# An attention and mixture-of-experts block on one core: shared-expert tiles read x from the router's transposed copy, 18 of them placed ahead of the routed tiles and 14 behind, and late pairs stored plainly

## What is computed

```python
x = x + attn(layernorm(x))                       # 32 heads of 16 features, plus a memory read
h = layernorm(x)
scores = sigmoid(h @ router_w.T)                 # 16 experts
_, topk_idx = top_k(scores + e_bias, 4)
topk_w = scores[topk_idx] / sum(scores[topk_idx])
routed = sum over the 4: topk_w * (silu(g) * u) @ down.T      with g, u = h @ gate_up.T (192 each)
shared = silu(h @ shared_gate.T) * (h @ shared_up.T) @ shared_down.T
out = x + routed + shared
```

## Time and profile before

| | us |
|---|---|
| median of 3 runs (1951.1 to 1951.97) | 1951.28 |
| the profiled execution | 1949.25 |
| its span, from first to last instruction | 1947.2 |
| attention alone (to the first `gate_up` at 1098.25) | 1098 |
| pairs 0 to 9 | 98 |
| routed pairs 10 to 81 | 674 |
| late pairs, joins and last stores | 77 |

### The profile page before, as it was taken

How to read it: one execution, slowest core, us unless ns; L and a number is a source line. 1 busy time by engine, 2 the same in 40 slices (tenths; PEclk the granted TensorE clock), 3 DMA queues, 4 the chain that set the end, 5 groups by cost and what they waited for, 6 DMA issues and landing times.

```text
span 1947.2 us, 34879 instructions
## 1 busy us (share of the span) xinstructions
PE 1870.6 (96%) x9240; PEld 965.5 (50%) x9241; DVE 1023.7 (53%) x1989; ACT 981.8 (50%) x1919; POOL 926.8 (48%) x1131
## 2 busy tenths in 40 slices
PE   6799999999999999999999899999999999999996
PEld 5444445444544454445333455555555555555553
DVE  5667777878787878787887152122211221222212
ACT  3366776677667767776776532223332232322321
POOL 3532566666667766774643550333333333333333
PEclk9799999999999999999999999999999999999998
DMA  6423234534453345333542797777777777777779
GB/s 193 111 67 83 64 95 131 149 98 107 130 151 100 104 129 153 100 96 114 150 148 72 275 343 231 183 142 141 141 143 144 141 141 142 145 141 144 140 163 218
DMA packets 158488, 275.61 MB, mean 142 GB/s; under 512 B 28640, under 2 KB 64736, under 8 KB 155552
## 3 DMA queue, kind: packets, MB, share of 16 engines
q0 software_dynamic: 41392, 106.96, 26.8%
q1 hardware_dynamic: 108688, 147.61, 26.6%
q10 hardware_dynamic: 8288, 19.58, 2.9%
HBM read 143.55 MB, written 136.27 MB: 144 GB/s over the span
## 4 chain that ended last, share of the span: by engine, by line
PE 86%; ACT 5%; DVE 3%; DMA 2%; issue 2%; SPq 1%; POOL 1%; DVEq 0%; POOLq 0%
PE ps_gu L1907 23%; PE ps_pv L1210 12%; PE ps_exp L1197 10%; PE ps_max L1183 9%; PE ps_y L1926 7%; PE ps_misc L1103 5%; PE ps_y L1930 5%; PE ps_x L1886 4%; ACT prob L723 3%; DVE mx L973 2%; PE ps_misc L1128 2%; PE ps_misc L1152 2%; PE ps_misc L1223 1%; PE ps_misc L1074 1%; PE ps_misc L1117 1%
## 5 line engine op out<-in xcount | busy, mean ns | idle before, releaser
L973 DVE TENSOR_REDUCE mx<-ps_max 128x2 f32<-128x1024 f32 x512 | 618.1, 1219 | 172.5 <-PE ps_max L1183 158.5
L723 ACT ACTIVATE prob<-ps_exp 128x512 f32<-128x512 f32 x1024 | 583.9, 597 | 154.1 <-PE ps_exp L1197 136.6
L1197 PE MATMUL ps_exp<-qs,ks 98*128 98x512 bf16 x1024 | 391.8, 384 | 24.0 <-ACT prob L723 19.9
L1907 PE MATMUL ps_gu<-wts_sb,xT 128*128 x1152 | 402.7, 493 | 1.3 <-issue 1.1
L1611 POOL DMA_INDIRECT out<-yt,idx x72 | 111.9, 1554 | 467.8 <-ACT yt L1680 453.7
L1183 PE MATMUL ps_max<-ks,qs 96*128 96x512 bf16 x1024 | 308.7, 383 | 9.0 <-DVE mx L973 4.9
L1784 DVE COPY hT<-ps_h 128x384 f32<-128x384 f32 x88 | 49.1, 558 | 467.9 <-PE ps_h L1916 467.9
L1907 PEld LDWEIGHTS ps_gu<-wts_sb,xT 128*128 128x128 f32 x1152 | 207.3, 190 | 170.6 <-issue 56.1
L1210 PE MATMUL ps_pv<-prob,vs 128*32 128x512 f32 x2048 | 249.8, 601 | 0.0
L1670 ACT ACTIVATE gs<-ps_gu 128x192 f32<-128x192 f32 x176 | 58.3, 331 | 373.4 <-PE ps_gu L1907 373.4
L1197 PEld LDWEIGHTS ps_exp<-qs,ks 98*128 98x128 bf16 x1024 | 99.6, 98 | 209.3 <-ACT prob L723 101.3
(11 more groups left out here) (192 smaller groups left out, 2146.7 us busy)
## 6 DMA issues: line engine op xcount, KB each, us to landing
xt<-rows_by_expert SPq DMA_DIRECT2D x144, 264.5 KB, 2.8
dnr_sb<-in_dnr SPq DMA_DIRECT2D x144, 128.0 KB, 2.6
qk_parts<-parts POOLq DMA_DIRECT2D x112, 120.0 KB, 3.5
qs<-qk_parts SPq DMA_DIRECT2D x64, 192.0 KB, 3.1
wts_sb<-in_wts ACTq DMA_DIRECT2D x12, 1024.0 KB, 7.0
x_sb<-in_x SPq DMA_DIRECT2D x16, 512.0 KB, 4.5
qs<-qk_parts SPq DMA_DIRECT2D x64, 128.0 KB, 3.1
x_plus_memory<-am SPq DMA_DIRECT2D x16, 512.0 KB, 5.1
```

The source lines that it names most:

```text
L723: act.activation(prob[:, s, q], ps_exp[:, q % 2], ACT.Exp, scale=SCALE).then_inc(s_exp, 1)
L973: dve.tensor_reduce(mx[:, k % 2, 4 * s + 2 * p:4 * s + 2 * p + 2], ps_max[:, p], AX_X, ALU.max).then_inc(s_maxd, 1)
L1197: pe.matmul(ps_exp[:, q % 2], ks[0:ROWS + MROWS, kk, s * P:(s + 1) * P], qs[0:ROWS + MROWS, kk, q], start=True, stop=True).then_inc(s_sc, 1)
L1907: mm = pe.matmul(ps_gu[:, i, 0:2 * I], xT[:, i, d], w, start=(d == 0), stop=(d == DC - 1))
```

## The change

`xn2T` gets the layout [partition, tile, chunk, column] and SP stores it (`store_xn2T`) into a new area `xn2_transposed` in place of the rows of `xn2`. Shared tiles load x from there, already transposed, and `gate_up` takes it from `xt` directly. The transposes of x on PE and the copies on ACT are left out for the 16 shared pairs. The slot of x is free only when `gate_up` has read it, so `load_x` now waits for `gate_up` of the pair (`s_gu`) tile by tile, where it waited for the pair's transposes. ACT may write `xn2T` of the next unit only after the store of this one has landed: a new wait in `xn2T_out`, and POOL's wait in `norm2` goes. `EARLY` is 18: pairs 0 to 8 are early, 9 to 80 routed, 81 to 87 late, seven of them. The weights of experts 12 and 13 move from pair 8 to pair 7. The constants `jrow` are loaded at pair 4 and not 3. Of the late pairs only the first adds into `out` in DRAM. The other six load both sums (12 loads of 512 KB where there were 5), DVE adds them (`both_sums`, before for the last pair only), and ACT stores the result (`store_late`). Joins are 10 where there were 12.

```diff
-EARLY = 20
+EARLY = 18
...
-    xn2T = lent("xn2T", [P, DC, UT])
+    xn2T = lent("xn2T", [P, 2, DC, P])
...
+        def store_xn2T(c):
+            wait(s_xn2T, 2 * c + 2)
+            sp.dma_start(XN2T[c], xn2T[:, :, :, :].rearrange("p t c j -> p t (c j)")).then_inc(s_xn2st[c % 2], 16)
...
+                if k == 0 and b >= 4:
+                    store_xn2T(b - 4)
+                if k == 2 and b == NB:
+                    store_xn2T(NU - 3)
...
-                    if b >= 3:
-                        store_xn2(b - 3)
...
-                store_xn2(NU - 2)
                 store_x2(NU - 1)
+                store_xn2T(NU - 2)
             if n == 2:
-                store_xn2(NU - 1)
+                store_xn2T(NU - 1)
...
-                wait(s_xn2st[c % 2], 16 * (c // 2))
...
+                if t == 0 and c > 0:
+                    act.wait_ge(s_xn2st[(c - 1) % 2], 16 * ((c - 1) // 2) + 16)
+                    act.sem_inc(s_acf, 1)
                 act.wait_ge(s_xn2Tp, 2 * c + t + 1)
-                act.activation(xn2T[:, :, t * P:(t + 1) * P], ps_misc[:, :].rearrange("p (c t) -> p c t", c=DC),
+                act.activation(xn2T[:, t], ps_misc[:, :].rearrange("p (c t) -> p c t", c=DC),
...
-            self.summed = known and h >= H1 + 2
+            self.both = known and h > H1
...
-    WEIGHTS_AT = {0: 2, 1: 3, 2: 4, 4: 5, 8: 6, H0 + 3: 7}
+    WEIGHTS_AT = {0: 2, 1: 3, 2: 4, 4: 5, 7: 6, H0 + 3: 7}
...
-        def load_x(pair):
+        def load_x(last, pair):
+
             for i in range(2):
+                if last.exists and last.kind == SHARED:
+                    wait(s_gu, 2 * last.h + i + 1)
                 if pair.kind == SHARED:
-                    sp.dma_start(xt[:, pair.slot(i), 0:D], XN2[bass.ds(pair.t[i], 1)].rearrange("o p d -> (o p) d")).then_inc(
-                        s_x[pair.slot(i)], 16)
+                    sp.dma_start(xt[:, pair.slot(i), 0:D], XN2T[pair.t[i] // 2, :, i]).then_inc(s_x[pair.slot(i)], 16)
...
-                wait(s_xp, 2 * pair.h + 2)
                 if pair.kind == ROUTED:
+                    wait(s_xp, 2 * pair.routed + 2)
...
-                load_x(later)
-            for n, h in enumerate((0, 1, 2)):
+                load_x(pair, later)
+            for n, h in enumerate((0, 1, 3)):
                 if is_at(pair, h):
                     chain(n)
-            if is_at(pair, 3):
-
-                all_of("logits", "x2_stored", "o_added")
+            if is_at(pair, 4):
+
+                all_of("logits", "x2_stored", "xn2_stored", "o_added")
...
-        def load_sum(o, n, to, s):
+                           max_dma_last_dim=8192).then_inc(s, 16)
+
+        def load_sums(n):
             t = EARLY + 2 * n
-            pool.dma_start(sums[:, to], SUM[o][t * P:(t + 2) * P].rearrange("(t p) d -> p t d", p=P)).then_inc(s, 16)
-
-        def add_late(pair):
-            if not pair.summed:
-
-                wait(s_join[pair.h - H1], 16)
+            for o in range(2):
+                rows = SUM[o][t * P:(t + 2) * P].rearrange("(t p) d -> p t d", p=P)
+                pool.dma_start(sums[:, (LATE // 2) * o + n], rows).then_inc(s_sl[n], 16)
+
+        def add_first_late(pair):
+            wait(s_join[0], 16)
             for i in range(2):
                 wait(s_y, 2 * pair.h + i + 1)
-                pool.dma_start(rows_of(SUM[0], pair.t[i]), late_y(pair, i), accum_op=ALU.add).then_inc(s_lst[pair.slot(i)], 16)
+                pool.dma_start(rows_of(SUM[0], pair.t[i]), late_y(pair, i), accum_op=ALU.add).then_inc(s_lst[i], 16)
 
         wait(s_yp, H1)
-        load_sum(1, 2, 2, s_sl[2])
-        for n in range(2):
-            join(EARLY + 2 * n, n)
-        load_sum(1, 3, 3, s_sl[3])
-        for m in range(LATE // 2 - 1):
-            for t in (4 * m, 4 * m + 2):
-                join(t, 2)
-            if m == 1:
-                for n in range(4, LATE // 2):
-                    load_sum(1, n, n, s_sl[n])
-            if m == 2:
-                load_sum(0, LATE // 2 - 1, 0, s_sl0)
-            add_late(Pair(H1 + m, (H1 + m) // 2, (H1 + m) % 2))
+        load_sums(1)
+        join(EARLY, s_join[0])
+        load_sums(2)
+        early = iter(range(0, EARLY, 2))
+        for n in range(3, LATE // 2):
+            for t in (next(early), next(early)):
+                join(t, s_join[1])
+            if n == 4:
+                add_first_late(Pair(H1, H1 // 2, H1 % 2))
+            load_sums(n)
+        for t in early:
+            join(t, s_join[1])
...
+        def store_late(pair):
+            for i in range(2):
+                act.wait_ge(s_y, 2 * pair.h + i + 1)
+                act.sem_inc(s_acg, 1)
+                act.dma_start(rows_of(SUM[0], pair.t[i]), late_y(pair, i)).then_inc(s_last, 16)
...
-            if following.exists:
+            if following.exists and following.kind == ROUTED:
...
-            if before.exists and not before.summed:
+            if before.exists and not before.both:
...
+            if before.both:
+                store_late(before)
...
-        x_out(Pair(0, 0, 0))
...
+        def both_sums(pair):
+            n = pair.h - H1
+            dve.wait_ge(s_sl[n], 32)
+            dve.tensor_tensor(sums[:, n], sums[:, n], sums[:, LATE // 2 + n], ALU.add).then_inc(s_both, 1)
...
-            if pair.h == H2 - 1:
-                dve.wait_ge(s_both, 1)
-            else:
-                dve.wait_ge(s_sl[n], 16)
+            dve.wait_ge(s_both, n)
...
-            if before.exists and before.summed:
+            if before.both:
+                both_sums(before)
                 y_sum(before)
```

73 lines of the change are left out of this document (32 added, 41 removed).

## The result

The changed kernel takes 1965.05 us (median of 4 runs, 1962.89 to 1965.81); the kernel before took 1951.62 in the same session (4 runs, 1951.1 to 1953.33). The ratio is 1.0067, with a 95% interval of 1.0056 to 1.0079: slower by 0.67%, where I had forecast 0.17% and a range that ended at 1962. The profiled execution is the one of 1962.89 us; its span is 1961.1, 13.9 more than before (1947.2).

A forecast was written before the change was run, and what follows sets the result against it. PE was taken to bound the kernel, except before the first routed pair (x behind pads) and at the end (POOL's queue). Early stage 0, routed -1.8, end +5.0: +3.2 us, 1952.5 profiled, 1954.5 against the median; range 1945 to 1962.

The forecast's parts named there:

- Transposes cost 0.88 us a pair: Shared pairs on PE: the eight transposes of x take 0.88 us for each pair, 14.1 us over 16 pairs.
- If PE alone set the early stage, the first routed gate_up would come at 1182.4: Early stage, bound by PE only: first routed gate_up at about 1182.4, a gain of 14; said not to be reached.
- SP starts its pads at about 1151 and the second group at 1160: Early stage, SP's queue: pads wait behind pair 5's gate_up, starting at about 1151, not 1147.9; second group at 1160.
- Weights 12 and 13 push the last pads back by 5 us: Early stage: 2.1 MB of weights on ACT's queue delay SP's last pads by about 5 us, to 1186.
- A clock of 0.5 costs 2.5 us: Before the first routed gate_up: after PE's wait the granted clock falls to 0.5, costing 2.5 us.
- Early stage: 0: Up to the first routed gate_up, forecast at 1196.5: gain 0, with bounds of 14 and -3.
- Attention: 1 us: Attention, unit 13: ACT's copy waits for unit 12's store and PE waits for ACT; 1 us taken.
- Routed part and what follows it: -1.8: 72 routed pairs at the same pace; 0.9 us earlier to the first late pair, 0.9 more to the last routed addition.
- End: +5.0: After the last routed addition: 2.6 us more DMA work and 2.4 us more tail; the end grows by 5.
- weights do not hold the pads: Rival, early stage: pads not delayed, clock stays; first routed gate_up at 1189 to 1191, kernel 1947 to 1949; chance 0.18.
- late pairs at PE's pace: Rival, end: late pairs go at PE's pace, end 3 shorter instead of 5 longer, 1946.5; chance 0.12.
- the third rival: End: DVE waits early for sums and PE behind it; end grows by 10 to 13, 1959.5 to 1962.5; chance 0.18.

The follow-up runs named there:

- a_early20: Changed kernel with the split of the kernel before, 20 shared tiles early and 12 late, plain late stores kept; ratio 1.0005 to the kernel before.
- a_all: Changed kernel with weights 4 and 5 later, weights 12 and 13 at pair 8, pads ahead of x loads, ten PE instructions; 1944.34 us, ratio 0.9963.
- a_weights_later: Changed kernel, but ACT sends the weights of experts 4 and 5 after the first silu of pair 1; 1968.31 us, ratio 1.0051 to the kernel before.
- a_pads_first: Changed kernel, but on SP the six pads of pairs 5 and 6 stand ahead of the loads of x for pairs 7 and 8; ratio 1.0051.
- a_weights8: Changed kernel, but the weights of experts 12 and 13 are sent at pair 8, not pair 7; ratio 1.0015 to the kernel before.

## Why the routed pairs take 5 us more

PE's loop does the same work in both kernels; its code differs only in how it waits and in the registers for that. What differs is where it lies: its first instruction is PE's 14168 before and 14030 after. So I moved it, with instructions at the very start of PE's program that only count up a semaphore:

```
         def _(pe):
+            for _ in range(10):
+                pe.sem_inc(s_steps, 1)
             experts["tensor"](pe)
```

> The changed kernel with 10 more instructions at the very start of PE's program, which only count up a semaphore that nobody reads. They move the loop of routed pairs in PE's instruction stream from instruction 14030 to 14040; in the kernel before it begins at 14168, and both 14168 and 14040 leave the same rest when divided by 128. Theory: the 0.1 to 0.45 us that PE loses at the top of nearly each of the 32 passes (7.9 us over the routed part, 1.8 in the kernel before) hang on where the loop's code lies in memory. Then the routed part falls from 679.1 to 673 to 675 us and the time to about 1959.5. Rival: they come from what the loop holds now (waits counted from the first routed pair need other registers) or from another engine; then the routed part stays 679 and the time 1965.

Routed part 672.5 us, 6 pairs late by 1.0 us together. The loss is gone, with ten instructions *added*. PE's waits from 1210 to 1870 in this run:

```profile
PE ps_gu L1919 <- issue: 0.3, 1, 0.3
```

The time was 1964.02 us against 1959.94 on its chip (I had expected 1959.5), ratio 1.0013 (0.9998 to 1.0027), where the changed kernel had 1.0067. The early stage of the profiled execution happened to be 3.9 us longer than in the changed kernel (residual at +21.0, POOL's wait for `xm_sb` 7.5 us for 6.1), for which I have no reason.

The other side of the test is to make the kernel before slow.

> The kernel before with 6 more instructions at the start of PE's program, which only count up a semaphore nobody reads; its loop of routed pairs then begins at PE's instruction 14174 instead of 14168, so that the rest by 16 is 14, as in the changed kernel (14030), where it was 8. In the changed kernel the loop cost 7.9 us at 14030 and 1.0 at 14040. Theory: it is the place of the loop's code, whatever the kernel, and what counts in it is the place within a piece of 16 instructions. Then the routed part grows from 673.9 to 678 to 680 us and the time by about 5 us. Rival: the place within a larger piece counts (14174 leaves 30 by 64 and 94 by 128, 14030 leaves 14 and 78), or the loss needs the changed kernel's loop; then the routed part stays within 1.5 us of 673.9.

Six instructions (14174) did nothing: 673.6 us, ratio 0.9995 (0.9983 to 1.0006), so it is not the place within 16 instructions, as I had thought. With 118 the loop begins at 14286:

> The kernel before with 118 counting instructions at the start of PE's program: its loop begins at PE's instruction 14286, which leaves 78 by 128, as 14030 in the changed kernel does. With 6 (14174) the routed part had stayed 673.6 us, so a rest of 14 by 16 is not what makes the loop slow. Theory: the place within a piece larger than 16 instructions counts, whatever the kernel. Then the routed part grows to 678 to 680 us, with 25 or more of 72 pairs late. Rival: the loss needs what the changed kernel's loop holds, together with its place; then 672 to 675 us.

Routed part 680.2 us, 28 pairs late by 8.0 us together, time 1966.25 against 1950.1: ratio 1.0089 (1.0068 to 1.0109). Only 6.2 of the 16 us are the loop. About 8 are the counting instructions themselves: PE's first matmul began at 18.96 us and not at 11.05, behind "issue" and no longer behind DVE, and the attention ended 9.8 us later. (With 6, 10 and 64 of them, in b_pe6, a_pe10 and a_pe64, it still began at 10.8 to 10.9.) The kernel *before*, with nothing changed in its work, has the changed kernel's loss in the loop. Its PE waits from 1210 to 1870:

```profile
PE ps_gu L1907 <- issue: 5.5, 22, 0.6
```

The first matmul, PE's timeline in this run and in the kernel before:

```profile
18.96 1.09 PE L1255 MATMUL ps_misc<-identf,xn 128*128 128x128 f32 x4 [18.96 <-issue]
```
```profile
11.05 1.09 PE L1255 MATMUL ps_misc<-identf,xn 128*128 128x128 f32 x4 [11.05 <-DVE xn L1008]
```

> The changed kernel with 64 counting instructions at the start of PE's program: its loop begins at PE's instruction 14094, which leaves 14 by 64 as 14030 does, but 14 by 128 where 14030 leaves 78. Theory (pieces of 64 instructions or of a part of 64): routed part 678 to 680 us, as without them. Rival (pieces of 128 or more, or a few hot places only): 672 to 675 us.

At 14094 the routed part took 673.2 us: the theory that a rest by 64 decides it is refuted. In all, of the places of the loop's start, 13988, 14040, 14094, 14168 and 14174 gave 672 to 674 us in ten profiled executions, 14030 and 14286 gave 678 to 680 in eight. The two slow ones lie exactly 256 apart. The Trainium skill, "Advanced Engine Details and Errata", section "ISA Cache", says that a sequencer's instruction cache has lines of 256 instructions. By that rule both slow places are the same place in a line (206) and each fast one is another (164, 216, 14, 88, 94), with which the runs agree. They do not single out 256: counted by 128 the two slow places are alike as well (78), and no fast one is (36, 88, 14, 88, 94). Nor does the rule say why 206 is slow and 216 is not, when the loop of 219 instructions crosses a line's end from both, and no run here tells that. Shown is that the place alone makes and removes the loss; what in the place does it stays open.

## What the end waits for

**Without the joins of the early tiles.** Nine joins are left out, so the rows of the early tiles in out lack their second sum.

```
             for t in (next(early), next(early)):
-                join(t, s_join[1])
+                pass
...
-        for t in early:
-            join(t, s_join[1])
```

> The changed kernel without the nine joins (out += second sum, 0.5 MB each) of the early tiles, which POOL issues among the loads of sums: it leaves these additions out, so the early tiles' rows of out lack their second sum. It measures what the end of the kernel waits for. Theory: from POOL's first load of a sum to the end (60.7 us) the transfers on POOL's queue set the time, joins among them; without them DVE no longer waits 20 us for sums, and the stretch falls to what PE needs for the seven late pairs, 50 to 53 us, the time to 1954 to 1957. Rival: the sums come as late without the joins, because the loads' own bytes and the routed additions set them; then it stays at 58 us or more.

From the first load of a sum to the end it took 50.0 us, 10.7 less, and the one wait of DVE for a sum there is 0.3 us. The time was 1953.69 us, ratio to the kernel before 1.0021 (1.0010 to 1.0032). So it is the joins, and the loads of sums behind them on POOL's queue, that set the last 60 us of the changed kernel; PE's pace would allow 50.

```profile
DVE wts_sb L1836 <- DMA wts_sb<-second_sum_rows: 0.3, 1, 0.3
```

**Split and stores apart.** In three executions (before, b_pe6, b_pe118) the late code of the kernel before took 58.2, 60.2 and 60.1 us, so the 2.5 of the two first profiles say little. Four kernels on one chip, the two splits with either late stage. The old late stage is put back word for word (joins and accumulating stores for the first two late pairs, accumulating stores over one loaded sum for the next, both sums for the last); its core:

```
-        load_sums(1)
-        join(EARLY, s_join[0])
-        load_sums(2)
+        load_sum(1, 2, 2, s_sl[2])
+        for n in range(2):
+            join(EARLY + 2 * n, n)
+        load_sum(1, 3, 3, s_sl[3])
...
+            add_late(Pair(H1 + m, (H1 + m) // 2, (H1 + m) % 2))
```

> The changed kernel once more, on one chip with the next three: split 18/14, plain late stores. The theory that the bytes and kinds on POOL's queue set the late stage (joins 0.203, loads 0.375 MB a us): 60 to 61.5 us from POOL's first load of a sum to the end, with the old late stage at the same split 1 to 3 us more (PE needs seven pairs, and eleven joins' and twelve additions' work comes to 31 us more than its loads). Rival: the late code makes no difference at all, 0.5 us or less between the two.

> The changed kernel with the late stage of the kernel before at the split 18/14: two late pairs added by joins and accumulating stores, five over sums, all accumulating but the last pair. Theory of POOL's queue: 11 joins and 12 accumulating additions of 0.262 MB are 8.9 MB at 0.203, 43.9 us, and its 6 loads of sums, 6 of x and 2 stores 5.2 MB at 0.375, 14 us: 57.9 us, as much as the plain one (57.7), so 60 to 62 us to the end. Rival (the plain stores cost): under 59 us.

> The changed kernel with 20/12, plain late stores, on the same chip: 11 joins and 2 additions accumulate (6.3 MB, 31.0 us), 10 loads of sums, 5 of x, 10 stores are plain (9.2 MB, 24.5 us): 55.5 us, 2.2 less than at 18/14. Theory: the stretch to the end is 1 to 2 us shorter than in after_2. Rival: a late pair less gives PE's 8.5 us, over 5.

> The changed kernel with 20/12 and the late stage of the kernel before: the work on POOL's queue is that of the kernel before, 55.1 us, so by the theory the stretch is within 1 us of that of a_early20_2. Rival: PE's late pairs without transposes (8.47 for 9.34 us) end it earlier: 3 us or more shorter.

From the first load of a sum to the end:

| | plain late stores | the old late stage |
|---|---|---|
| 18 and 14 | 61.2 (after_2) | 64.3 (a18_old_late) |
| 20 and 12 | 59.6 (a_early20_2) | 60.8 (a20_old_late_2) |

An earlier run of the last one gave 60.9:

> The changed kernel with the split 20 and 12, and with the late stage of the kernel before put back (two late pairs added by joins and accumulating stores, one load of a sum each for the next, two for the last): against the run with 20 and 12 alone it takes the plain late stores away. PE's loop begins at the same instruction (13988) in both. There the routed additions' end (POOL's first load of a sum, 1899.5) to the end of the span was 59.7 us with 15.3 less of PE's work, and in the kernel before 58.2. Theory: that stretch is set by the bytes and kinds of POOL's transfers, not by PE. Then it takes 58 to 59 us here, though PE's pairs take 8.47 us where they took 9.34, so the plain stores cost about 1.2 us. Rival: PE's shorter pairs let the old late stage end earlier; the stretch takes 54 us or less, and the plain late stage has cost over 5 us.

That run had been forecast at 58 to 59 us, with the plain stores as a cost of 1.2; its time was 1959.47 us, ratio 1.0045 (1.0030 to 1.0061), where a_early20 had 1.0005. So the plain stores are a gain, 3.1 us at the split for which they were made and 1.2 at the other, and the split costs 1.6 with them (3.5 without). The 64.3 is one execution, 2.3 above the highest of nine with plain stores. At 20 and 12 it is two against two (60.8 and 60.9 against 59.6 and 59.7), where the forecast had them within 1. Which of the kernels ends how is seen at PE: with the old stage at 18 and 14 it is through at 1948.4, 18 us before the end, while POOL's last additions went out at 1944.84 only; with the plain one it is through at 1956.2, 5 us before. PE's last row in each:

```profile
1947.29 1.13 PE L1947 MATMUL ps_y<-sdnr_sb,hT 64*128 64x512 f32 x4
```
```profile
1954.10 2.08 PE L1942 MATMUL ps_y<-sdnr_sb,hT 64*128 64x512 f32 x4
```

My estimate of equal work for the two at 18 and 14 (57.9 against 57.7 us, so 60 to 62 to the end) missed that an accumulating store can only be sent when its y is there: POOL stood idle for 5.9 and 6.7 us ahead of its last two pairs of them, waiting for DVE.

## Both kernels beaten

The three edits on the pads and the ten instructions together:

> All four together on the changed kernel: weights of experts 4 and 5 after the first silu of pair 1, weights 12 and 13 at pair 8, pads ahead of the loads of x, 10 instructions ahead on PE. Theory: singly they gave 5.8, 6.0 and (forecast) 5 us of the wait for the pads and 6.6 us of the routed part; the three on the pads overlap, since PE's shared pairs end about 82 us after the end of attention and the first routed gate_up can't be earlier than 86. So the first routed gate_up at 88 to 94 us after the end of attention, the routed part 672 to 674, and the time 0.5 to 1 per cent below the kernel before. Rival: x for pair 8, now behind the pads, becomes late and PE waits for it; then the first routed gate_up stays at 98 or more and the time within 0.3 per cent of the kernel before.

1944.34 us against 1949.92 of the kernel before on the same chip: ratio 0.9963, interval 0.9952 to 0.9973, 9 and 25 runs. Span 1942.9. The first routed `gate_up` comes at +90.9, 15.7 us earlier than in the changed kernel (13.1 against the earliest of its five) and 7.0 to 9.1 earlier than before the change; PE has no wait for routed x left. Its timeline shows the two waits that remain in the early stage:

```profile
1170.74 4.50 PE L1923 MATMUL ps_gu<-sgu_sb,xt 128*128 128x384 f32 x8 [5.00 <-DMA xt<-xn_transposed]
...
1182.48 2.85 PE L1923 MATMUL ps_gu<-sgu_sb,xt 128*128 128x384 f32 x8 [1.56 <-DMA xt<-xn_transposed]
...
1192.00 2.85 PE L1923 MATMUL ps_gu<-wts_sb,xT 128*128 x8
```

To take these two away I mixed loads and pads: one tile of x, three pads, the other tile, three pads.

```
                     for e in range(POOL_PADS + 6 * n, POOL_PADS + 6 * n + 6):
+                        if e % 3 == POOL_PADS % 3:
+                            load_x(pair, later, [(e - POOL_PADS) // 3 % 2])
                         pad(e)
-                    load_x(pair, later)
```

> The run with all four, with SP's order in pairs 5 and 6 once more changed: a load of one tile of x, three pads, the other tile, three pads. With all six pads ahead PE waited 5.0 and 1.6 us for x of pairs 7 and 8, and its first routed gate_up came 90.9 us after the end of attention, 7.7 after SP's load for it. Theory: these two waits stand on PE's way there; with x loaded earlier they go, the pads keep within 2 us of their times (48.7 and 57.2), and the first routed gate_up comes at 87 to 89, the time 2 to 4 us shorter. Rival: the load for the first routed pair (83.2) is set by the pads and comes 2 to 3 us later now; then the gate_up stays at 90 to 92 and the time the same.

It did not help, as the rival said, and came out worse than the rival too: the last three pads went out at +69.2 and the load of routed x at +84.6 (rival: 2 to 3 us later than +83.2), PE still waited 2.2 and 2.1 us for x of shared pairs and now 3.9 for routed x, the first routed `gate_up` came at +94.1 (rival: 90 to 92), and the time was 1948.4 us, ratio 0.9993 (0.9984 to 1.0003) for 0.9963. Of the two orders, six pads ahead is the better.

## Why the prediction was wrong, step by step

- *Transposes cost 0.88 us a pair.* Right. Shared pairs went at 8.46 to 8.47 us, routed ones at 9.34.
- *If PE alone set the early stage, the first routed gate_up would come at 1182.4.* It was never reached, as the prediction said. a_all, the nearest to it, had it at +90.9, which is 1187.6 counted from the changed kernel's end of attention.
- *SP starts its pads at about 1151 and the second group at 1160.* **The step that failed first.** They started at 1156.36 and 1168.26. The forecast moved pair 5 by the transposes alone, to about 1145; it began at 1149.08. It had put what the missing copies of x free on ACT at nothing ("ACT does not bind"), and had not looked at what ACT sends earlier for it, nor at what the new waits for `gate_up` do to SP's queue ahead of pair 5: together they put 2 MB of weights ahead of the load of `xm_sb`, which then took 11.8 us for 4.3 (3 to 6 us at the first routed `gate_up`, a_weights_later). And it took the wait for `gate_up` as one delay, of the first group; in fact a load of x stands ahead of each group and waits anew (3 to 5 us, a_pads_first).
- *Weights 12 and 13 push the last pads back by 5 us.* Right in kind, and 7.1 in size on the load of routed x (a_weights8). The turn by packets that the Trainium skill, "DMA: Bandwidth & Descriptors", section "Queues, rings and completion order", states, if it meant half of the time for each queue, would have made 3; the measurement decides.
- *A clock of 0.5 costs 2.5 us.* The two parts of `down` took 3.62 and 1.62 for 1.88 and 1.13 us at the full clock, 2.2 more; with two groups of transposes of 1.1 us each for 0.66, 3.1 in all. Near.
- *Early stage: 0.* It was +6.6. The forecast had the load of routed x going out at 1186.5, and it went out at 1192.66, 6.2 later; from there to the `gate_up` it took 10.6 us, for 10.0 forecast. So nearly the whole error lies ahead of that load, in the pads.
- *Attention: 1 us.* It was 0.15, by a forecast whose mechanism is in the trace: at 1062 ACT waits 3.4 us for the store of unit 12 and PE 1.4 us for ACT, and the wait of 1.0 us for `qs<-mT` that PE had before is gone. With attentions that end up to 9.5 us apart, a single pair of executions can't tell the size.
- *Routed part and what follows it: -1.8.* It was +4.7. The -0.9 of the last pair is in it; what was not foreseen is 6 us by the place of PE's loop in its program (late pairs: 7.8 us together against 1.6). No row of the trace before could show that. Ten instructions more ahead of the loop take it away (a_pe10), and 118 bring it to the kernel before (b_pe118).
- *End: +5.0.* It was +2.5 in the first two profiles, and less against the other executions of the old late code (60.7 against 60.1 and 60.2). The sum over bytes was right in telling that the end would not get shorter and that DVE would wait for sums. What was mis-sized is the tail: the last sums were there 55.2 us after POOL's first load (forecast 53), but from DVE's last addition to the end it took 2.8 us, where the forecast had a store of 3 to 4 and 2.7 behind it. The last store on SP's queue landed in 2.0.
- *The rivals.* None came true. That weights do not hold the pads is refuted by a_weights8; late pairs at PE's pace by the 20.8 us of DVE's waits, though a_no_early_joins shows that pace (50.0 us) once the joins are gone. DVE did wait for sums, five times in the seven late pairs, as the third rival said, but the end grew by 2.5 us and not 10 to 13.

The sum of what was shown: 6.6 + 5.2 - 0.5 + 2.5 + 0.15 = 13.9 us. Some 6 of these (5.2, and the 0.9 that the routed part should have gained) have nothing to do with the work that the change moves; without them the kernel would have taken some 1959 us, still 4.5 above the forecast: most of it is the early stage's 6.6 less the 2.5 by which the end stayed below its forecast.

## What to carry to other kernels

Work taken off an engine that binds nothing still moves what this engine sends, and a new wait on one queue moves what stands behind it there, so look at which transfers of the two change places, and at who waits for them. A buffer that is read by the consumer itself, and not by a copy ahead of it, comes free a step later; on an in-order queue everything behind its next load waits too, so put what someone else waits for (here the pads) ahead. And before a loop's slowdown is put down to a change, move the loop by a few dummy instructions and time it again, and look in the profile whether these cost time themselves, as the 118 did.

## What the runs showed of the hardware that I had not expected

- The place of a loop's code alone cost some 6 us in 674: mostly 0.1 to 0.46 us at the top of most of the 31 or 32 passes, at two of seven places, in both kernels, shown by PE as idle time that ended with "issue".
- Two weight transfers of 1 MB, started a microsecond ahead of a load of 0.5 MB, made it take 11.8 us for 4.3. From 1106 to 1110 ACT's queue had 85.5% of the engines and SP's 13.6% (queues of that stretch in the changed kernel: packets, MB, share), 7.5 KB a packet against 1.8:

```profile
q10 hardware_dynamic: 177, 1.32, 85.5%
q1 hardware_dynamic: 118, 0.21, 13.6%
```

- 118 instructions that only count up a semaphore, at the start of PE's program, put its first matmul off from 11.05 to 18.96 us (b_pe118); 64 of them did not move it (10.91, a_pe64).
